# The steps of the final layer norm stand elsewhere in a pass, and a layer's value weights are fetched ahead of the shifted state

## The reference, cut to what matters

```python
x = L0_attn_x                                                     # 16 sequences x 256 tokens x 128
x = _layernorm(x + _L0_attn_ref(x, ...), axis=-1)                 # state space layer
x = _layernorm(x + _L0_ffn_ref(x, ...), axis=-1)                  # mixture of experts
x = _layernorm(x + _L1_attn_ref(x, ...), axis=-1)                 # a second state space layer
x = _layernorm(x + _L1_ffn_ref(x, Wqkv, ...), axis=-1)            # six transformer layers

def _L1_ffn_ref(x, Wqkv, q_scale, k_scale, Wo, ln_g, ln_b, W1, b1, W2, b2):
    for i in range(DEPTH):                                        # DEPTH = 6
        x = attn_layer(shift_tokens(x), Wqkv[i], q_scale[i], k_scale[i], Wo[i]) + x
        x = ffn_layer(shift_tokens(x), ln_g[i], ln_b[i], W1[i], b1[i], W2[i], b2[i]) + x
    return x
def attn_layer(x, Wqkv, qs, ksc, Wo):   # 16 heads of 64, q and k normalized and rotated, windows of 32
    ...
def _layernorm(x, axis=-1, eps=1e-05):
    m = jnp.mean(x, axis=axis, keepdims=True)
    v = jnp.var(x, axis=axis, keepdims=True)
    return (x - m) / jnp.sqrt(v + eps)
```

## Time and profile before

| | us |
|---|---|
| median of three runs | 4003.33 |
| profiled execution, its own time | 4004.87 |
| its span, first to last instruction | 4003.1 |
| PE busy | 3757.7 (94%) |
| DVE busy | 3069.1 (77%) |
| POOL busy | 2370.9 (59%) |
| ACT busy | 2194.8 (55%) |

### The profile page before, as it was taken

The page is one execution under the profiler, slowest core; times in us unless marked ns, Lnnn a source line. Parts: engine busy times, 40 slices in busy tenths (PEclk is TensorE's granted clock), DMA queues, the critical chain, the costliest instruction groups (busy, mean ns, idle before and its releaser), DMA issues.

```text
span 4003.1 us, 149191 instructions
## 1 busy us (share of the span) xinstructions
PE 3757.7 (94%) x67429; PEld 2633.4 (66%) x67429; DVE 3069.1 (77%) x5081; ACT 2194.8 (55%) x3295; POOL 2370.9 (59%) x1692
## 2 busy tenths in 40 slices
PE   5999999977899999999999999999999999989886
PEld 3776777664566666666666666666666666666664
DVE  5434444455888898999899898998988989987773
ACT  3111111043566666677667666767766767765563
POOL 2001000015777777777777777777777777776672
PEclk8999999998999999999999999999999999999997
DMA  4111111000000000000000000000010000000000
GB/s 164 43 43 64 43 43 47 38 1 5 11 11 11 13 27 22 13 11 16 23 23 11 12 23 21 17 14 11 22 30 11 11 14 27 22 13 14 14 12 12
DMA packets 50655, 98.35 MB, mean 25 GB/s; under 512 B 11611, under 2 KB 40678, under 8 KB 45542
## 3 DMA queue, kind: packets, MB, share of 16 engines
q1 hardware_dynamic: 49286, 88.42, 7.0%
q10 hardware_dynamic: 736, 0.40, 0.0%
HBM read 61.25 MB, written 2.36 MB: 16 GB/s over the span
## 4 chain that ended last, share of the span: by engine, by line
PE 62%; DVE 4%; POOL 4%; issue 3%; ACT 3%; DMA 1%; SPq 0%; POOLq 0%; DVEq 0%; ACTq 0%
PE pQ L1737 16%; PE pW L1775 8%; PE pW L1719 7%; PE pW L1760 6%; PE pC L1835 6%; PE pM L1786 4%; PE pW L1786 4%; PE pM L1800 4%; PE pW L1800 4%; PE pC L1845 3%; POOL rot L1311 1%; POOL rot L1319 1%; PE pC L1820 1%; DVE m L1451 1%; DVE rot L1441 1%
## 5 line engine op out<-in xcount | busy, mean ns | idle before, releaser
L1319 POOL TENSOR_TENSOR rot<-rot,m 128x1024 f32<-128x1024 f32 x384 | 908.2, 2365 | 363.9 <-DVE m L1451 363.9
L1586 ACT ACTIVATE sq<-pQ 128x1024 f32<-128x1024 f32 x380 | 389.3, 1025 | 639.8 <-PE pQ L1737 622.7
L1311 POOL TENSOR_TENSOR rot<-rot,rn 128x1024 f32<-128x1024 f32 x384 | 728.8, 1909 | 7.5
L1441 DVE TENSOR_TENSOR rot<-pQ,tabl 128x1024 f32<-128x1024 f32 x380 | 463.5, 1220 | 113.3 <-ACT sq L1586 113.3
L1463 DVE TENSOR_REDUCE n<-sq 128x16 f32<-128x1024 f32 x380 | 461.4, 1214 | 114.8 <-ACT sq L1586 113.7
L1451 DVE TENSOR_TENSOR m<-pQ,tabl 128x1024 f32<-128x1024 f32 x380 | 461.1, 1214 | 3.7 <-POOL rot L1319 3.7
L597 POOL TENSOR_TENSOR b_xcT<-b_cB,b_xT 128x2048 f32<-128x2048 f32 x16 | 72.2, 4514 | 604.8 <-DMA b_cB<-b_crow 563.2
L1737 PE MATMUL pQ<-wk,xs 128*128 128x512 f32 x760 | 380.1, 622 | 10.1 <-DVE m L1451 5.7
L1737 PE MATMUL pQ<-wq,xs 128*128 128x512 f32 x760 | 380.9, 624 | 5.8 <-DMA xs<-XT 3.3
L1348 POOL TENSOR_TENSOR E<-E,rc 128x1024 f32<-128x1024 f32 x192 | 361.4, 1904 | 25.7 <-DVE rc L1423 25.7
L1775 PE MATMUL pW<-oT,wo 128*128 128x256 f32 x1536 | 361.8, 390 | 4.1 <-ACT oT L1606 4.1
(11 more groups left out here) (240 smaller groups left out, 6854.6 us busy)
## 6 DMA issues: line engine op xcount, KB each, us to landing
b_cB<-b_crow SPq DMA_DIRECT2D x32, 1024.0 KB, 6.1
xs<-XT SPq DMA_DIRECT2D x192, 64.0 KB, 2.6
ys<-XT SPq DMA_DIRECT2D x192, 64.0 KB
wq<-in_wqkv SPq DMA_DIRECT2D x6, 512.0 KB, 3.6
wk<-in_wqkv SPq DMA_DIRECT2D x6, 512.0 KB, 4.7
wv<-in_wqkv SPq DMA_DIRECT2D x6, 512.0 KB, 4.8
wo<-in_wo SPq DMA_DIRECT2D x6, 512.0 KB, 4.7
w<-in_w SPq DMA_DIRECT2D x6, 384.0 KB, 4.0
```

The lines of the kernel that those rows point to most:

```text
L1311: e.tensor_tensor(r, r, rn[b % 2][:, c:c + HEADS].unsqueeze(2).to_broadcast([P, HEADS, HD]), ALU.mult)\
L1319: e.tensor_tensor(rot[j % RING][:, :], rot[j % RING][:, :], m2[:, :, :].rearrange("p h d -> p (h d)"), ALU.add)\
L1441: e.tensor_tensor(heads(rot[j % RING][:, :]), heads(projected(j)), tabl[n // NSEQ % 2][:, t, 2 * w, :].unsqueeze(1).to_broadcast([P, HEADS ...
L1586: e.activation(squared(j), projected(j), ACT.Square).then_inc(a_sq.sem, 1)
```

## The change

Two things are moved; no instruction is added, removed or altered.

```diff
@@ SyncE, once a pass @@
+                if R is not None and starts(R + 1) and R + 1 < NP:
+                    e.wait_ge(p_v.sem, p_v.passed(R + 1))
+                    e.dma_start(wqkv[2][:, :], I["wqkv"][(R + 1) // NSEQ, :, 2 * N:3 * N]).then_inc(wqkv_l[2], 16)
                 if Dn is not None:
                     fetch_ys(Dn)
                     if starts(Dn + 1) and Dn + 1 < NP:
                         e.dma_start(wo[:, :, :], ...)
-                if R is not None and starts(R + 1) and R + 1 < NP:
-                    e.wait_ge(p_v.sem, p_v.passed(R + 1))
-                    e.dma_start(wqkv[2][:, :], ...)
@@ GpSimd @@
                 unit_scale(R, 2)
-                last_root(F)
                 rotary_add(A, 2)
                 by_sum(B, 0)
+                last_root(F)
                 by_sum(B, 1)
@@ VectorE @@
                 normal(C)
-                last_stats(F)
                 squares(A, 1)
...
                 sums(B, 0)
+                last_stats(F)
                 sums(B, 1)
@@ ScalarE @@
                 exponents_again(C)
-                last_normal(F)
                 exponent(B, 0)
...
                 turned(R, "2a")
+                last_normal(F)
                 turned(R, "3b")
@@ TensorE @@
                 project(A, 1)
-                last(F)
                 turn(R, "0a")
...
                 attend(Dn, 3)
+                last(F)
                 project(A, 3)
                 turn(R, "2a")
                 turn(R, "2b")
```

More of the change, by code:

```diff
@@ L1281, in _ @@
                         e.dma_start(wo[:, :, :], I["wo"][(Dn + 1) // NSEQ, :, :, :]).then_inc(wo_l, 16)
-                if R is not None and starts(R + 1) and R + 1 < NP:
-                    e.wait_ge(p_v.sem, p_v.passed(R + 1))
-                    e.dma_start(wqkv[2][:, :], I["wqkv"][(R + 1) // NSEQ, :, 2 * N:3 * N]).then_inc(wqkv_l[2], 16)
                 if F is not None:
```

## The result

| | before | after |
|---|---|---|
| median, us (4 runs each, beside each other) | 4002.3 | 3944.12 |
| all runs, us | 3999.38 to 4005.74 | 3940.41 to 3953.98 |
| profiled execution, us | 4004.87 | 3942.75 |
| span, us | 4003.1 | 3940.9 |
| ratio, 95% interval | | 0.9863 (0.9845 to 0.988) |

A forecast was written before the change was run, and what follows sets the result against it. PE's own work was taken to bound the kernel, PE being 94% busy. F passes 55.0, drain 4.5 and `wv` 6.0 us sum to 65.5 us, taking the profiled 4004.87 to 3939.4, so a median of 3938 us; range 3927 to 3956.

The forecast's parts named there:

- The F passes: Passes 85 to 96, with the final normalization beside everything else: from 35.20 to 30.20 us each, 55.0 us won over 11.
- The clock's share: PE's lower clock in the F passes: 1.82 us a pass, left over from 5.22, was to go.
- The step that was mis-sized: DVE's `last_stats`, 1.20 us, in front of the second sum: cost put at 0, ends -0.1 and +0.83 us a pass.
- PE's step: `last(F)` in front of PE's projection: waits for nothing late, shifts what follows by 0.22 us for two transposes.
- POOL's and ACT's: `last_root` behind POOL's first division and `last_normal` before ACT's last copy of keys: cost 0, ACT's slack 0.6 us.
- `wv`: Value weights fetched early by SP: PE's five waits for them go, 6.0 us won, bounds 0 and 7.5.
- Drain: From pass 96 on: waits for X and in front of the exponentials go, 4.5 us won, ends 3.4 and 6.5.
- Thin cover: Rival: DVE's 0.83 us or a late `fsh` reaches PE each pass, 9 us, median 3947; chance 13%.
- `wv` wins nothing: Rival: PE may wait for instructions instead where the transfer now runs, median 3944 to 3949; chance 8%.
- the wait for X keeps the clock down: Rival: the wait moves to `turn(R, "2b")`, 0.6 us, clock stays low; 27 us over 11 passes, 3965; chance 5%.
- The slower case: Rival: `fsh` so late that ACT's last copy of keys, which `scores` needs, waits; median 4010; chance 3%.

The follow-up runs named there:

- e3: The kernel before with only ACT's `last_normal(F)` moved to its new place, in front of the last copy of keys; 3955.89 us, ratio 0.9882.
- e10: The changed kernel with ACT held by four copies of the mask in front of `oT` in each F pass; 3993.54 us, ratio 0.9973.
- e2: The kernel before with only the value weights fetched early, the final normalization where it was; 3995.0 us, ratio 0.9985.
- e5: The changed kernel with DVE making the statistics of X twice in each F pass, at the same place; 3955.25 us, ratio 0.9881.
- e11: The kernel of e4 run once more, on one chip with e12; 3942.65 us, ratio 0.9853.
- e4: The changed kernel with `last_stats` cut in two, the statistics put behind the addition of the attention output; 3940.87 us, ratio 0.9849.
- e7: The changed kernel run once more, unaltered; 3946.15 us, ratio 0.9853.
- e12: The changed kernel run once more, unaltered, on one chip with e11; 3940.15 us, ratio 0.9853.
- e1: The changed kernel with the value weights fetched at their old place, so only the four normalization steps moved; 3948.14 us, ratio 0.9873.
- e8: The kernel before with ACT's `last_normal(F)` moved and the value weights fetched early, the other three steps unmoved; 3946.02 us, ratio 0.9857.
- e9: The changed kernel with ACT held by two copies of the mask in front of `oT` in each F pass; 3953.16 us, ratio 0.9877.

## Why the prediction was right

**The F passes: right, 4 us too much.** The forecast took 5.00 us from each of 11 passes, 55.0 us; the profile shows 50.8. The cause was the one named, ACT waiting for `fsh` in front of the exponentials: e3 takes that away alone and wins 52.9 us. The clock's share was put at 1.82 us a pass as a remainder. In the change itself 50.8 us are 31.3 + 3.6 us of waits gone, less 3.9 of new ones and 2 more of `issue`, which leaves 22 us, 2.0 a pass, and PE's busy time for the same instructions fell by 21.6. e10 shows 1.25 us a pass for a somewhat shorter stop. But the size belongs to one execution: against e2 PE's busy time falls by only 15.0 us, 1.4 a pass. The forecast's working with e2's stretch in place of that of the kernel before gives 381.1 - 11 x 30.20 = 48.9 us, an estimate, and not 55.0.

**The step that was mis-sized** is DVE's: "It catches up before PE needs it. I put this at 0". DVE does catch up before PE's projections (0.7 us of waits even in e5, with twice the statistics). But what is left of its delay, 0.6 us by the forecast's own reckoning, also stands in front of the addition of the attention output, and the fetch of `ys` hangs on that. PE waited 2.9 us for `ys`, where nothing was forecast. Ahead of the mark of pass 87 the addition starts at 3560.02 in the kernel after, and SP's second half of `ys` at 3560.94. The timeline of SP there:

```profile
3560.94 0.60 SPq L1248 DMA_DIRECT2D ys<-XT  x1
```

PE's mark, the use of `ys`, came 3.44 us after that, at 3564.38, without a wait; in pass 95 and 96, from the second halves at 3806.48 and 3837.04, it came only after 3.81 and 3.78 us, with waits of 0.55 and 2.32 us. The transfer's time varies by more than the room that is left: 1.9 to 3.7 us to landing in e11. e4 and e5 show DVE's part by both signs.

**PE's step**: `last(F)` "waits for nothing late" was nearly right; it waited 1.0 us over 11 passes. The two transposes cost 0.27 us a pass, 0.22 was taken. **POOL's and ACT's** steps cost nothing, as forecast.

**`wv`: right.** 6.0 us were forecast; the five intervals are 6.6 us shorter (156.3 and 149.7). **Drain**: 4.5 us were forecast, 5.1 measured (105.2 us from the mark of pass 96 to the end before, 100.1 after; 106.8 in e2, 99.4 in e7 and 98.3 in e12).

**What the sum missed by.** In the profiles 62.2 us are gone: 50.8 + 5.1 in and behind the F passes, 3.1 from the mark of pass 5 to that of 85, 3.2 ahead of pass 5, where nothing was changed. The 3.1 are the 6.6 of `wv` less 3.5 of other stops; one of these in pass 32 is the largest. There PE waited 1.91 us for `issue` and then ran at the low clock; the timeline of PE in the kernel after:

```profile
1927.58 3.78 PE L1737 MATMUL pQ<-wk,xs 128*128 128x512 f32 x4 [1.91 <-issue]
1931.16 1.06 PE L1786 MATMUL pW<-ident,rot 128*128 128x128 f32 x4
```

The kernel before waited 2.2 us at the same instruction and ran it in 1.98 us, at the full clock; e1, which fetches `wv` at the old place, waits 2.1 us for `issue` in the same pass, so the stop is not the early fetch's. Such things differ from run to run, and they spread the medians: the three medians of the changed kernel lie 6 us apart. Of the 7 us between forecast and measured gain about 4 lie in the F passes, where 2.9 us of waits for `ys` are shown; the rest can't be told from scatter, that of the profile that the forecast was worked out from among it.

**The rivals.** Thin cover was the nearest, with another victim than the one named: not PE's projections but `ys`. That `wv` wins nothing fell with e2, that the wait for X keeps the clock down with e3 and e8. The slower case did not come: ACT kept its slack, but only 0.16 to 0.70 us of it in the passes 85 to 95, 0.29 in most.

## What to carry to other kernels

When a step of a minor chain stands in one engine's list ahead of work that the bound engine waits for, look for the idle time just ahead of an instruction that is waiting for the bound engine anyway, and put it there; here one such move on one engine gave nearly all, and the moves on the other engines only exchanged a small wait for another. When a step is put into an engine's list, follow every reader of what stands behind it up to the next use, the transfers that other queues issue for it too: idle time per pass says nothing about the room in front of one instruction. A weight fetch in an in-order queue belongs at the place where its buffer comes free, not behind a fetch that waits for the end of the pass.

## What the runs showed of the hardware

Stops of PE had a price beyond their length only when they were long, and not each time. In the F passes of e9 stops of up to 0.7 us for `oT` left the transposes behind them at 0.60 us and the granted clock at 1.00. Of the stops for `oT` of 2.7 to 3.2 us in the kernel before, nine of ten were followed by the lower clock; of those of 2.8 to 3.2 us in e2, whose steps there are the same, seven of eleven; of those of 2.2 to 2.6 us in e10, eight of nine. The timeline of PE in e2, pass 93, has a stop of 3.23 us with the transposes behind it at full speed:

```profile
3809.96 0.63 PE L1786 MATMUL pW<-ident,rot 128*128 128x128 f32 x4 [3.23 <-ACT oT L1606]
3810.42 0.60 PE L1786 MATMUL pM<-ident,rot 128*128 128x128 f32 x4
```

A stop of 2.36 us in e10, shown above, had them at 1.09. Waits for `issue` went either way too: one of 2.2 us left the next projection at 1.98 us in the kernel before, and one of 1.91 us at the same instruction was followed by 3.78 us in the kernel after. So the length of a stop alone does not tell its price; what else decides was not found. With the clock, a wait of 2.85 us a pass cost 4.7 to 4.8 us in the kernel before, and one of 3.08 us cost 4.4 in e2 (3.08 and 1.4 of busy time).
